# Attention and mixture of experts on one core: the fifth score tile of each unit laid over its two PSUM banks as 384 and 256 columns

## The chip, the cores and the metric

The kernel runs on one core of a Trainium2 chip. The metric is the device time of one execution, in microseconds, as the median of several runs. The program has one launch and no arithmetic on the host beyond repacking of weights. TensorE is PE below, its weight loads are PEld, VectorE is DVE, ScalarE is ACT, GpSimd is POOL, SyncE is SP.

## What is computed

A layer norm feeds two branches, whose sum is added to the input: causal attention with rotary positions (2 batches, 1024 tokens, 16 heads of 128), and a mixture of 32 experts with a shared expert, which takes the same normalised tokens. The change touches the attention's scores alone. Cut to what matters:

```python
q = rope((x @ wq.T + bq).reshape(b, s, 16, 128))        # b = 2, s = 1024
k = rope((x @ wk.T + bk).reshape(b, s, 16, 128))
v = (x @ wv.T + bv).reshape(b, s, 16, 128)
attn = jnp.einsum('bihd,bjhd->bhij', q, k) * scale
attn = jnp.where(causal[None, None], -jnp.inf, attn)     # j > i is masked
attn = jax.nn.softmax(attn, axis=-1)
o = jnp.einsum('bhij,bjhd->bihd', attn, v).reshape(b, s, 2048)
y = o @ wo.T + bo + residual
```

## The kernel before

**Units.** One head of one batch is a unit; there are 32 (`UNITS`), numbered n, and the program is a loop over them after a prologue (layer norm, transposes, the shared expert, the gate). In the loop every engine has its work written out by hand in a fixed order, and semaphores tie the engines together. The stages of neighbouring units overlap: while the scores of unit n are made, the second half of unit n-1 is weighted with its values and projected out, and the rotary inputs of unit n+1 are projected. From unit 13 on, sixteen units also carry a pair of experts each (`expert_turn`, `expert_up`, `expert_down`).

**Precision by three products.** Most operands are held as a high and a low part, and `three` (L284 to L287) issues three matmuls for one product: high by high (L285), high by low (L286), low by high (L287). Each of these has its own weights, so every matmul comes with a weight load. In the rows a group by L285, L286, L287 of the same width is one such product. The rows name the stationary and the moving operand after the arrow; the form ends in the number of columns that are moved, so `128x384` is 384 columns.

**Scores.** A unit has eight score tiles, t = 0 to 7. Tile t holds 128 queries against the (t + 1) x 128 keys that the causal mask lets through. `scores` (L383) makes it in PSUM. A PSUM bank holds 512 columns of 4 bytes; `score[0]` is banks 0 and 1 joined, `score[1]` banks 2 and 3, and tile t lies in `score[t % 2]` from column 0 on. One matmul can't cross a bank, so tiles 0 to 3 are one piece and tiles 4 to 7 are two: 512 columns in the first bank, and 128, 256, 384 or 512 in the second. Behind the pieces a bf16 matmul (L399) adds the mask to the last 128 columns and signals `s_done`.

**What follows a tile.** DVE takes the negated maximum of each row over the whole tile (L1388, `nmax`), ACT the exponential with it as bias and the row sum (L959, `prob`), then PE transposes `prob` in groups of up to four blocks (L409, `turn`) into one of four ring banks (banks 4 to 7, `take`), from which ACT makes the high part (L970, `ptd_h` or `ptr_h`) and DVE the low one (L1397). These are the moving operands of `weighted`. The score tile t waits for the exponential of tile t - 2, which empties its banks.

**The order on PE around tile 4.** In unit n it is: the second half of unit n-1 is weighted, in the expert units the gathered tokens are transposed (`expert_turn`, L456), then `scores(n, 4)`, `project(n + 1, 2)`, `turn(n, 3)`, `project(n + 1, 3)`, `scores(n, 5)`, `outproj(n - 1, 1, 0)`, `turn(n, 4)`, `scores(n, 6)`.

**The rotary chain.** `project` makes q and k of the next unit; ACT copies them with their bias into `qb` (L759, L763); SP swaps their two halves by DMA into `qs` (`swap`); POOL multiplies with cosine and sine and adds (L1525, L1526, L1529); ACT and POOL or DVE make high and low parts (L772, L1073). `scores(n, 0)` and `scores(n, 4)` wait for them.

Of the kernel before, what the change touches and what calls it, by code (L numbers as in the profile page):

```python
# [10 lines left out]
ALU = mybir.AluOpType  # L11
ACT = mybir.ActivationFunctionType
AX = mybir.AxisListType

P = 128
# [4 lines left out]
TILES = SEQ // P  # L20
CH = 512
# [61 lines left out]
def layer(nc, x, wqk, wvp, wop, biases, epack, gate_wt, gate_bias, sh_gate, sh_up, sh_down, cols, bo_row, cst, out):  # L83
# [9 lines left out]
    with ExitStack() as ctx:  # L93
        def sb(name, shape, dt=F32, where=ctx):
            return where.enter_context(nc.sbuf_tensor(name, shape, dt))
# [3 lines left out]

        ps = ctx.enter_context(nc.psum_tensor("ps", [P, 8, CH], F32))  # L100
        score = [ps[:, 2 * i:2 * i + 2, :].rearrange("p a b -> p (a b)") for i in range(2)]

        k_sb = sb("k_sb", [P, C_END])
        ident, cos_sb, sin_sb = k_sb[:, C_ID:C_ID + P], k_sb[:, C_COS:C_COS + SEQ], k_sb[:, C_SIN:C_SIN + SEQ]
# [2 lines left out]
        bias = sb("bias", [P, 3 * HEADS])  # L107
# [71 lines left out]
        prob = sb("prob", [P, 2, SEQ])  # L179
        nmax, rsum, rinv = sb("nmax", [P, TILES]), sb("rsum", [P, TILES]), sb("rinv", [P, TILES])  # L180
# [103 lines left out]
        def three(eng, dst, lhs, rhs, start, stop):  # L284
            eng.matmul(dst, lhs[0], rhs[0], start=start, stop=False)  # L285
            eng.matmul(dst, lhs[0], rhs[1], start=False, stop=False)  # L286
            return eng.matmul(dst, lhs[1], rhs[0], start=False, stop=stop)  # L287

        @block.tensor
        def _(pe):  # L290
# [92 lines left out]
            def scores(n, t):  # L383
                if n not in range(UNITS):
                    return
                if n == 0 and t in (0, 1, 4, 5):
                    i = 2 * (t % 2) + t // 4
                    pe.wait_ge(pro_free[i], len([u for u in range(len(pro_uses)) if u % 4 == i]))
                if not (n == 0 and t < 2):
                    pe.wait_ge(exp_done, TILES * n + t - 1)  # L390
                if t % 4 == 0:
                    pe.wait_ge(rope_l, 4 * n + (2, 4)[t // 4])
                s = n % 2
                dst, i = score[t % 2], slice(t * P, (t + 1) * P)
                for c in range(t // 4 + 1):
                    w = min(CH, (t + 1) * P - c * CH)
                    j = slice(c * CH, c * CH + w)
                    three(pe, dst[:, j], (q_h[s][:, i], q_l[s][:, i]), (k_h[s][:, j], k_l[s][:, j]), True, c < t // 4)
                pe.matmul(dst[:, t * P:(t + 1) * P], maskb[:, 0:P], maskb[:, P:2 * P], start=False,  # L399
                          stop=True).then_inc(s_done, 1)  # L400
# [157 lines left out]

            for n in range(UNITS):
                scores(n, 0)  # L560
                turn(n - 1, 8)
                turn(n - 1, 9)
                if n > 1:
                    values(n - 1, 2)
                scores(n, 1)
                if n > 1:
                    values(n - 1, 3)
                turn(n - 1, 10)
                expert_down(n - 1)
                turn(n - 1, 11)  # L570
                project(n + 1, 1)
                scores(n, 2)
                masks(n, 0)
                bias_row(n)
# [227 lines left out]
        def _(act):  # L802
# [151 lines left out]
            def exps(n, t):  # L954
                if n not in range(UNITS):
                    return
                act.wait_ge(max_done, TILES * n + t + 1)
                w = (t + 1) * P
                act.activation(prob[:, t % 2, 0:w], score[t % 2][:, 0:w], ACT.Exp, bias=nmax[:, t:t + 1],  # L959
                               accum_out=rsum[:, t:t + 1]).then_inc(exp_done, 1)  # L960

            def turned_hi(n, g):
# [46 lines left out]
            for n in range(UNITS):  # L1009
                g = n // 4  # L1010
                exps(n, 0)
                turned_hi(n - 1, 11)
                expert_out(n - 1)
                exps(n, 1)
                rope_in(act, n + 1, 1)
                masks(n, 0)
                bias_row(n)
                turned_hi(n, 0)
                turned_hi(n, 1)
                masks(n, 1)  # L1020
                exps(n, 2)
                rope_hi(act, n + 1, 0)
                turned_hi(n, 2)
# [79 lines left out]
        def _(dve):  # L1103
# [280 lines left out]
            def maxes(n, t):  # L1384
                if n not in range(UNITS):
                    return
                dve.wait_ge(s_done, TILES * n + t + 1)
                dve.tensor_reduce(nmax[:, t:t + 1], score[t % 2][:, 0:(t + 1) * P], AX.X, ALU.max,  # L1388
                                  negate=True).then_inc(max_done, 1)

            def turned_lo(n, g):
# [59 lines left out]
            for n in range(UNITS):  # L1451
                g = n // 4
                if n == 1:
                    dve.memset(ones[:, :], 1.0).then_inc(ones_ready, 1)
                maxes(n, 0)
                if n > 1:
                    v_lo(dve, n - 1, 2)
                maxes(n, 1)
                if n > 1:
                    v_lo(dve, n - 1, 3)  # L1460
                turned_lo(n - 1, 10)
                turned_lo(n - 1, 11)
                add_out(n - 1, 0, 0)
                turned_lo(n, 0)
                maxes(n, 2)
                add_out(n - 1, 0, 1)
                add_rest(n, 0)
# [219 lines left out]
```

## Time and profile before

| what | us |
|---|---|
| median of 3 runs | 1086.73 |
| the three runs | 1086.23, 1086.73, 1088.49 |
| the profiled execution | 1089.67 |
| its span, from the first instruction to the last | 1087.8 |
| PE busy in it | 1046.8 (96%) |
| POOL, DVE, ACT busy in it | 749.5, 719.7, 658.6 |

The profiled execution is one execution of its own, with a span from the first to the last instruction; the numbers of the trace are of this one. The busy time of PE is modelled at its end: a matmul's shown duration holds its way through the array, and successive matmuls overlap. How long a full PE takes for a matmul is the distance between the starts of two rows. The chain of work is a list of pieces, each from the time at which its releaser was done.

### The profile page before, as it was taken

Reading aid. Unit: us, or ns where it says so; the run is one execution under the profiler, and the core shown is the slowest. Engines: PE = TensorE matmul, PEld = TensorE weight load, DVE = VectorE, ACT = ScalarE, POOL = GpSimd, SP = SyncE. Lnnn points to the kernel's source line nnn. Section 1 sums busy time; section 2 is a strip of 40 time slices with the busy share of each in tenths; the row PEclk is TensorE's granted clock in tenths of the full one; section 3 lists DMA queues with packets and bytes.
Section 4 is the critical chain, followed back from the end, with each engine's and each line's share of the span. In section 5 each row is a group of like instructions: output and inputs, shape, how many; then the busy total and the mean of one; then the engine's idle time right before and its main releaser. Section 6 shows DMA issues by size and latency. Waiting matters only on the chain.

```text
span 1087.8 us, 19027 instructions
## 1 busy us (share of the span) xinstructions
PE 1046.8 (96%) x6738; PEld 917.8 (84%) x6738; DVE 719.7 (66%) x1489; ACT 658.6 (61%) x1448; POOL 749.5 (69%) x654
## 2 busy tenths in 40 slices
PE   3999999999999999999999999999999999999996
PEld 3888888888878888888988888898888889888885
DVE  5867778778778766656665565666566556656575
ACT  3577656666665656656665566666556666656552
POOL 3826776767766575768678687867867877685751
PEclk9999999999999999999999999999999999999999
DMA  6221416212121211223332232332223232222112
GB/s 231 59 64 39 117 40 116 60 28 48 43 58 35 54 41 39 59 69 73 87 93 48 67 80 69 96 81 70 64 65 98 61 84 55 72 64 48 41 59 97
DMA packets 51629, 75.43 MB, mean 69 GB/s; under 512 B 12240, under 2 KB 29008, under 8 KB 51408
## 3 DMA queue, kind: packets, MB, share of 16 engines
q1 hardware_dynamic: 46144, 67.66, 23.7%
q0 software_dynamic: 5392, 6.56, 4.1%
q8 instruction: 55, 0.90, 0.4%
q14 instruction: 38, 0.31, 0.1%
HBM read 33.94 MB, written 10.90 MB: 41 GB/s over the span
## 4 chain that ended last, share of the span: by engine, by line
PE 79%; POOL 8%; DVE 4%; DMA 3%; ACT 3%; issue 2%; SPq 0%; DVEq 0%; POOLq 0%; ACTq 0%
PE ps L285 22%; PE ps L287 21%; PE ps L286 21%; PE ps L409 10%; PE ps L470 2%; DMA qs<-qb 2%; POOL qs L1526 2%; POOL qb L1529 2%; POOL qb L1525 2%; PE ps L399 1%; PE ps L482 1%; DMA fin_y<-token_sum 1%; DVE acc L1421 1%; POOL q_l L1073 1%; DVE nmax L1388 1%
## 5 line engine op out<-in xcount | busy, mean ns | idle before, releaser
L1525 POOL TENSOR_TENSOR qb<-qb,k_sb 128x512 f32<-128x512 f32 x128 | 170.9, 1336 | 236.3 <-DMA qs<-qb 235.9
L1388 DVE TENSOR_REDUCE nmax<-ps 128x1 f32<-128x128 f32 (+7 forms) x256 | 191.0, 752 | 63.9 <-PE ps L399 63.6
L959 ACT ACTIVATE prob<-ps,nmax 128x128 f32<-128x128 f32 (+7 forms) x256 | 190.3, 743 | 61.9 <-DVE nmax L1388 61.1
L970 ACT ACTIVATE ptd_h<-ps 128x128 fp32r<-128x128 f32 (+3 forms) x256 | 108.7, 436 | 191.1 <-PE ps L409 190.6
L1397 DVE TENSOR_TENSOR ptd_l<-ps,ptd_h 128x128 fp32r<-128x128 f32 (+3 forms) x256 | 124.6, 487 | 84.3 <-ACT ptd_h L970 81.4
L1529 POOL TENSOR_TENSOR qb<-qb,qs 128x512 f32<-128x512 f32 x128 | 165.8, 1295 | 19.0 <-POOL qs L1526 1.0
L409 PE MATMUL ps<-k_sb,prob 128*128 128x128 f32 x1152 | 172.7, 274 | 6.2 <-DVE ptr_l L1397 3.9
L1526 POOL TENSOR_TENSOR qs<-qs,k_sb 128x512 f32<-128x512 f32 x128 | 172.9, 1351 | 0.0
L409 PEld LDWEIGHTS ps<-k_sb,prob 128*128 128x128 f32 x1152 | 132.8, 141 | 18.5 <-issue 7.3
L285 PE MATMUL ps<-k_h,q_h 128*128 128x512 f32 (+3 forms) x384 | 140.9, 367 | 4.1 <-ACT prob L959 3.6
L1421 DVE SCALAR_TENSOR_TENSOR acc<-ps,rinv,acc 128x256 f32<-128x256 f32 x256 | 111.1, 476 | 33.9 <-PE ps L287 33.9
L287 PE MATMUL ps<-k_h,q_l 128*128 128x512 f32 (+3 forms) x384 | 132.7, 346 | 0.0
L286 PE MATMUL ps<-k_l,q_h 128*128 128x512 f32 (+3 forms) x384 | 132.6, 345 | 0.0
L285 PE MATMUL ps<-x2h,wqh 128*128 128x512 f32 x256 | 111.4, 435 | 5.4 <-DVE acc L1421 5.2
L287 PE MATMUL ps<-x2h,wql 128*128 128x512 f32 x256 | 100.7, 393 | 0.0
L286 PE MATMUL ps<-x2l,wqh 128*128 128x512 f32 x256 | 100.4, 392 | 0.0
L1397 DVE TENSOR_TENSOR ptr_l<-ps,ptr_h 128x512 fp32r<-128x512 f32 x128 | 87.6, 684 | 11.3 <-ACT ptr_h L970 11.0
L970 ACT ACTIVATE ptr_h<-ps 128x512 fp32r<-128x512 f32 x128 | 75.9, 593 | 21.4 <-PE ps L409 21.4
L285 PEld LDWEIGHTS ps<-k_h,q_h 128*128 128x128 f32 x384 | 72.5, 189 | 16.7 <-ACT prob L959 7.1
L1073 POOL TENSOR_TENSOR q_l<-qb,q_h 128x512 fp32r<-128x512 f32 x62 | 80.4, 1296 | 6.1 <-ACT q_h L772 5.8
L285 PE MATMUL ps<-ptd_h,v_h 128*128 128x512 f32 (+3 forms) x256 | 84.2, 329 | 0.0
L287 PE MATMUL ps<-ptd_h,v_l 128*128 128x512 f32 (+3 forms) x256 | 82.7, 323 | 0.0
(175 smaller groups left out, 2668.5 us busy)
## 6 DMA issues: line engine op xcount, KB each, us to landing
qs<-qb SPq DMA_DIRECT2D x256, 128.0 KB
ew<-epack SPq DMA_DIRECT2D x16, 768.0 KB, 4.3
rqk<-wqk SPq DMA_DIRECT2D x16, 256.0 KB, 3.0
xt<-x SPq DMA_DIRECT2D x4, 512.0 KB, 5.0
rv<-wvp SPq DMA_DIRECT2D x8, 256.0 KB, 3.3
ro<-wop SPq DMA_DIRECT2D x16, 128.0 KB, 2.3
token_table<-xn SPq DMA_DIRECT2D x4, 512.0 KB, 4.7
token_sum<-token_table SPq DMA_DIRECT2D x1, 2048.0 KB, 9.1
```

The source lines that it names most:

```text
L285: eng.matmul(dst, lhs[0], rhs[0], start=start, stop=False)
L286: eng.matmul(dst, lhs[0], rhs[1], start=False, stop=False)
L287: return eng.matmul(dst, lhs[1], rhs[0], start=False, stop=stop)
L409: ins = pe.transpose(bank[:, j * P:(j + 1) * P], prob[:, t % 2, (j0 + j) * P:(j0 + j + 1) * P], ident)
L959: act.activation(prob[:, t % 2, 0:w], score[t % 2][:, 0:w], ACT.Exp, bias=nmax[:, t:t + 1], accum_out=rsum[:, t:t + 1]).then_inc(exp_done, 1)
L970: act.activation(turned(0, t, j0, w), src, ACT.Copy).then_inc(pth_done, 1)
L1388: dve.tensor_reduce(nmax[:, t:t + 1], score[t % 2][:, 0:(t + 1) * P], AX.X, ALU.max, negate=True).then_inc(max_done, 1)
L1397: dve.tensor_tensor(turned(1, t, j0, w), src, turned(0, t, j0, w).bitcast(F32), ALU.subtract).then_inc(ptl_done, 1)
L1421: ins = dve.scalar_tensor_tensor(out=acc[:, t, :], in0=rbank("OP", u, c, i2)[:, i * DM:(i + 1) * DM], scalar=rinv[:, j:j + 1], in1=acc[:, ...
L1525: pool.tensor_tensor(qb[:, i, :], qb[:, i, :], cos_sb[:, c], ALU.mult).then_inc(rope_a, 1)
L1526: pool.tensor_tensor(qs[:, i % 2, :], qs[:, i % 2, :], sin_sb[:, c], ALU.mult).then_inc(rope_b, 1)
L1529: pool.tensor_tensor(qb[:, i, :], qb[:, i, :], qs[:, i % 2, :], ALU.add).then_inc(rope_t, 1)
```

## The change

The fifth score tile (t = 4, 640 keys) no longer starts at column 0 of its pair of banks but at column 128, and so takes columns 128 to 767: 384 in the first bank and 256 in the second, in place of 512 and 128. A list `tile` holds the view of each of the eight tiles; the others are where they were. `mid` is the number of columns of the first piece, 384 at t = 4 and 512 elsewhere. The maximum and the exponential read the new view. In `scores` the three matmuls of each piece take the widths that follow from it. No instruction is added, removed or moved.

```diff
+        tile = [score[t % 2][:, P * (t == 4):P * (t == 4) + (t + 1) * P] for t in range(TILES)]
...
-                dst, i = score[t % 2], slice(t * P, (t + 1) * P)
+                dst, i = tile[t], slice(t * P, (t + 1) * P)
+                mid = CH - P * (t == 4)
                 for c in range(t // 4 + 1):
-                    w = min(CH, (t + 1) * P - c * CH)
-                    j = slice(c * CH, c * CH + w)
+                    j = slice(c * mid, min((t + 1) * P, mid + c * CH))
                     three(pe, dst[:, j], (q_h[s][:, i], q_l[s][:, i]), (k_h[s][:, j], k_l[s][:, j]), True, c < t // 4)
...
-                act.activation(prob[:, t % 2, 0:w], score[t % 2][:, 0:w], ACT.Exp, bias=nmax[:, t:t + 1],
+                act.activation(prob[:, t % 2, 0:w], tile[t], ACT.Exp, bias=nmax[:, t:t + 1],
...
-                dve.tensor_reduce(nmax[:, t:t + 1], score[t % 2][:, 0:(t + 1) * P], AX.X, ALU.max,
+                dve.tensor_reduce(nmax[:, t:t + 1], tile[t], AX.X, ALU.max,
```

On PE, at the tile t = 4 of one unit, the order before has these rows (`k_h,q_h` and its like are keys moved against the stationary queries):

```order
L285 MATMUL ps<-k_h,q_h 128x512
L286 MATMUL ps<-k_l,q_h 128x512
L287 MATMUL ps<-k_h,q_l 128x512
L285 MATMUL ps<-k_h,q_h 128x128
L286 MATMUL ps<-k_l,q_h 128x128
L287 MATMUL ps<-k_h,q_l 128x128
L399 MATMUL ps<-maskb 128x128
```

and with the change, in the same place (its lines stand two further down):

```order
L287 MATMUL ps<-k_h,q_h 128x384
L288 MATMUL ps<-k_l,q_h 128x384
L289 MATMUL ps<-k_h,q_l 128x384
L287 MATMUL ps<-k_h,q_h 128x256
L288 MATMUL ps<-k_l,q_h 128x256
L289 MATMUL ps<-k_h,q_l 128x256
L401 MATMUL ps<-maskb 128x128
```

Only the widths differ, at all 32 tiles; the rows of the other engines keep their order and their forms.

## Rows read from the trace of the kernel before

**Rows 1.** The page, parts 1 and 2: PE's busy time, granted clock by slice

```profile
PE 1046.8 (96%) x6738; PEld 917.8 (84%) x6738; DVE 719.7 (66%) x1489; ACT 658.6 (61%) x1448; POOL 749.5 (69%) x654
...
PEclk9999999999999999999999999999999999999999
```

**Rows 2.** The page, part 4: shares of the chain that ended last

```profile
PE 79%; POOL 8%; DVE 4%; DMA 3%; ACT 3%; issue 2%; SPq 0%; DVEq 0%; POOLq 0%; ACTq 0%
```

**Rows 3.** Timeline of PE, unit 14, tile 4: start us, duration us, engine, line, tiles

```profile
511.94 0.48 PE L285 MATMUL ps<-k_h,q_h 128*128 128x512 f32 x1
512.25 0.40 PE L286 MATMUL ps<-k_l,q_h 128*128 128x512 f32 x1
512.49 0.39 PE L287 MATMUL ps<-k_h,q_l 128*128 128x512 f32 x1
512.72 0.22 PE L285 MATMUL ps<-k_h,q_h 128*128 128x128 f32 x1
512.77 0.28 PE L286 MATMUL ps<-k_l,q_h 128*128 128x128 f32 x1
512.89 0.27 PE L287 MATMUL ps<-k_h,q_l 128*128 128x128 f32 x1
513.00 0.23 PE L399 MATMUL ps<-maskb 128*128 128x128 bf16 x1
```

**Rows 4.** Timeline of the weight loads, the same tile, second piece

```profile
512.72 0.19 PEld L286 LDWEIGHTS ps<-k_l,q_h 128*128 128x128 f32 x1
512.83 0.19 PEld L287 LDWEIGHTS ps<-k_h,q_l 128*128 128x128 f32 x1
```

**Rows 5.** The chain in order of time (start us, us, what): one expert up projection

```profile
491.77 1.73 PE ps L470 x16
```

**Rows 6.** Timeline of PE, unit 14, tile 5: its first matmul, its second piece's, its mask

```profile
516.36 0.39 PE L285 MATMUL ps<-k_h,q_h 128*128 128x512 f32 x1
...
517.04 0.28 PE L285 MATMUL ps<-k_h,q_h 128*128 128x256 f32 x1
...
517.39 0.23 PE L399 MATMUL ps<-maskb 128*128 128x128 bf16 x1
```

**Rows 7.** Timeline of PE, unit 14, tile 2: its first matmul and its mask

```profile
503.56 0.33 PE L285 MATMUL ps<-k_h,q_h 128*128 128x384 f32 x1
...
504.08 0.23 PE L399 MATMUL ps<-maskb 128*128 128x128 bf16 x1
```

**Rows 8.** Timeline of ACT and of PE, unit 14: exponential of tile 4, its transposes

```profile
516.24 0.80 ACT L959 ACTIVATE prob<-ps,nmax 128x640 f32<-128x640 f32 x1
...
518.22 0.49 PE L409 MATMUL ps<-k_sb,prob 128*128 128x128 f32 x3
```

**Rows 9.** The chain in order of time, unit 3, around the routing work

```profile
179.87 0.69 DVE ol L1410
...
188.28 0.47 PE ps L285
```

**Rows 10.** The chain in order of time, unit 8

```profile
329.48 0.61 ACT oh L976
...
343.19 0.47 PE ps L285
```

**Rows 11.** The chain in order of time, last unit: the final additions

```profile
1051.34 1.14 DVE acc L1449
...
1069.36 1.15 DVE nmax L1388
```

**Rows 12.** The chain in order of time, unit 25 into 26: the rotary chain

```profile
872.97 3.58 DMA qs<-qb
...
887.35 0.30 ACT q_h L772
...
891.46 0.41 PE ps L409 x2
```

**Rows 13.** The chain in order of time, unit 0: another swap of the rotary halves

```profile
97.93 2.31 DMA qs<-qb
```

## Prediction

> **What bounds the kernel now.** I read four views, in this order. First the page: TensorE (PE) is busy for 96% of the span, at full granted clock in every slice [rows 1], so no clock effect hides in the time. Second, the chain of work that ended last: 79% of its length is PE [rows 2]. A busy share alone would prove little, since matmuls overlap in the trace and their ends are modelled; that the chain runs through PE is what makes a shorter PE stream worth something. Third, the timeline of PE around one fifth score tile (t = 4), in unit 14 [rows 3]. The reader is to look at the first column and not at the second: a matmul of 128 columns is shown with 0.22 to 0.28 us and one of 512 with 0.39 to 0.48 us, yet they start 0.23 us apart after a 512 and closer after a 128. What a matmul costs on a full PE is the distance from its start to the next start. Fourth, the chain in order of time, asked at each of the 32 tiles t = 4, to see which of them lie on it.
>
> **What 512 and 128 cost.** In [rows 3] the tile runs from 511.94 to its mask matmul at 513.00: 1.06 us. The three matmuls of 512 take 511.94 to 512.72, 0.78 us: 0.31 for the first, which follows transposes and has to make up for a late weight load, then 0.24 and 0.23. The three of 128 take 512.72 to 513.00, 0.28 us, in steps of 0.05, 0.12 and 0.11. A column costs 0.23/512 = 0.45 ns in the wide ones, so 128 columns are worth 0.06 us, and only the first of the three gets that. The other two stand at 0.11 to 0.12. The weight loads say why: the second and the third one of the narrow piece start at 512.72 and 512.83, 0.11 us apart [rows 4]. Each of these matmuls has its own weights, the next load can't start before the one ahead is done, and a matmul shorter than 0.11 us is waited out. That this floor doesn't come from the columns is shown elsewhere: 16 matmuls of the experts' up projection, 64 columns wide, take 1.73 us in one piece of the chain, again 0.108 us each [rows 5]. So some 0.11 us per tile are PE time in which no column moves.
>
> **What 384 and 256 cost.** Both widths stand in the trace of before. Three of 256, as the second piece of t = 5, take 517.04 to 517.39, 0.35 us or 0.117 each [rows 6]: just above the floor, so they hide their weight loads and pay almost only for their columns. Three of 384, the whole of t = 2, take 503.56 to 504.08, 0.52 us or 0.173 each [rows 7]. Of 512 three steady ones cost 3 x 0.233 = 0.70 by the steps of 0.24 and 0.23 in [rows 3]. The edits, for one tile:
> - first piece, 512 to 384: minus 0.70 - 0.52 = 0.18 us (the three of 512 in the tile t = 5 beside it run from 516.36 to 517.04, 0.68 [rows 6], by which it would be 0.16);
> - second piece, 128 to 256: plus 0.35 - 0.28 = 0.07 us;
> - the same six matmuls and six weight loads, the same 640 columns, the same mask of 128 columns at the end of the second bank, nothing moved in any engine's order: 0.
> Sum: minus 0.11, or minus 0.09 with the 0.16. I take 0.105, since 0.18 is what the steps beside the tile itself give, rounded down a little for the other end. The first matmul after transposes isn't seen with 384 columns and the short weights ahead. Its bounds: it shrinks by its columns (0.06, in the sum) or, if its 0.31 were all weight load, not at all, which would leave 0.045 per tile. I take the first, because it takes 0.08 more than a steady 512, and a fixed extra with the columns on top fits that; the low end is kept for the range.
>
> VectorE's maximum and ScalarE's exponential read the tile from column 128 to 768 in place of 0 to 640, over the same two banks. The form is the same 640 elements, and before, too, they step over a bank's end in the middle; I price this at 0. No row shows a read that begins inside a bank; if it cost something, the cover is this: the exponential of t = 4 runs from 516.24 for 0.80 us, and PE turns that tile from 518.22 on [rows 8], so over 1 us is free. Without this cover it would fall on the transposes' start.
>
> **How many of the 32 tiles count.** At 29 of them the chain consists of PE's matmuls of this very tile. The three others: in unit 3 the chain has gone to VectorE, with `ol` at 179.87 and then routing work up to PE's restart at 188.28 [rows 9], and the tile t = 4 stands beside it; in unit 8 it leaves PE for ScalarE's `oh` at 329.48, before the tile is done, and is back at 343.19 [rows 10]; in the last unit it runs over the final additions and their loads, from 1051.34 to 1069.36 [rows 11], with the tile beside them. There PE, being earlier, only waits longer. So the term is 29 x 0.105 = 3.05 us, and 32 x 0.105 = 3.4 would be the most.
>
> What is late next? The rotary chain: PE's projection, ScalarE's copy, the swap by DMA, GpSimd's products, ScalarE, PE. After the tile of unit 25 the chain takes that way, from the DMA at 872.97 to PE at 891.46 [rows 12]. The projections that start it stand behind the tile t = 4 in PE's order, and no other t = 4 stands between its start and its end, so an earlier tile moves the whole chain forward and the gain survives it.
>
> The sum is made against the profiled execution, 1089.67 us with a span of 1087.8, so 1.9 us lie outside and stay. It is 2.9 us above the median of the runs, about as far as the highest of them; the difference is carried over to the median: 1086.73 - 3.05 = **1083.7 us**, a ratio of 0.997.
>
> **Rivals.** (a) A matmul costs by its columns and nothing else. Then 3 x 640 columns stay 3 x 640 columns, and the time is 1086.7. For it: wide matmuls follow their columns closely. Against it: the steps of 0.11 and 0.12 for 128 columns [rows 3] and 0.108 for 64 [rows 5]. The Trainium skill has such a rule: TensorE: Matmul & The Clock Gate, section "Back-to-back issue gap", gives an isolated gap of columns / 2.4 plus 2.5 ns, by which both layouts cost alike; the same section says that weight loads push narrow matmuls above it, with 81 ns at 128 columns and 131 at 512, between which a straight line would again make the two layouts equal. The steps of 0.11 and 0.23 us here agree with neither pair, and the measurement decides.
> (b) Part of the gain ends in waits: a second path, nearly as long as the chain, that doesn't pass the tile. Where three units do this visibly, ten more might with the margin of a tenth of a microsecond; or the low bound of 0.045 per tile holds. 29 x 0.045 = 1.3, time 1085.4. For it: VectorE and ScalarE each form a queue in fixed order, and the chain visits them between units. Against it: the view of waits names no wait of a matmul in the stretch of the 16 expert units, so nothing there holds PE up now.
> (c) Slower: the swap of the rotary halves shares its queue with the experts' weights, the largest of the loads. It takes 3.58 us at 872.97 but 2.31 at 97.93 [rows 12, 13]. With PE a tenth earlier in each unit, swaps may meet loads that they missed before; ScalarE then stands at `q_h` until GpSimd is done, with the copies that PE needs queued behind it. The price is at most 3.58 - 2.31 = 1.27 us per unit. Two such units eat the gain, and from five on the kernel is slower by more than 2.2 us: 5 x 1.27 - 3.05 = 3.3, time 1090.0. Against it: the load is itself released by PE's steps, so the two keep their distance.
> (d) The widths aren't what the change says. The order of the built kernel shows 384 and 256 at the tiles and nothing else changed. 1086.7.
>
> **How the numbers follow.** Forecast 0.72; (a) 0.07; (b) 0.14; (c) 0.06; (d) 0.01. The bound of 0.2%, about what a measurement of this kernel can tell from no change, is 2.2 us, so faster means under 1084.6. The forecast's own range is 1082.6 (3.4 saved, and 0.7 of scatter, a little over the 0.5 between the two lower runs) to 1085.0; I put 0.65 of its 0.72 under 1084.6 and 0.07 above. Faster 0.65; same 0.07 + 0.14 + 0.07 + 0.01 = 0.29; slower 0.06. The range that should hold 8 in 10 runs from 1082.6 to 1086.4: it takes in (b) with its bound, and leaves out (c), most of (a) and (d), and the forecast's tails, together 0.18.
>
> **What would show it.** In the profile after: the tile t = 4 of unit 14 in about 0.95 us from first matmul to mask, with steps of 0.25, 0.17, 0.17, 0.12, 0.12, 0.12; its weight loads nowhere closer than the matmuls; the tiles' reads as long as before; the distance between the same tiles of neighbouring expert units shorter by 0.1 us. If the tile is shorter and the span isn't, it is (b), and new waits of PE stand behind ScalarE or VectorE. If the steps of 256 are above 0.12, or the 384s above 0.18, the sum per tile is wrong. Longer swaps at ScalarE's `q_h` would be (c).

## The result

| | median us | lowest to highest | runs |
|---|---|---|---|
| before | 1087.93 | 1085.24 to 1090.75 | 22 |
| after | 1085.33 | 1083.14 to 1087.09 | 22 |

The ratio is 0.9978, with a 95% interval of 0.997 to 0.9986: 2.4 us faster (1.5 to 3.3). The profiled execution of after has a span of 1083.6 us, 4.2 us less than that of before; that difference of two single executions holds more than the change, as is worked out further down.

The page of after, parts 1 and 4, against [rows 1, 2]:

```profile
PE 1043.6 (96%) x6738; PEld 918.5 (85%) x6738; DVE 720.2 (66%) x1489; ACT 659.0 (61%) x1448; POOL 748.9 (69%) x654
...
PE 84%; POOL 5%; DVE 4%; DMA 3%; ACT 2%; issue 1%; SPq 0%; DVEq 0%; POOLq 0%; ACTq 0%
```

PE's busy time is 3.2 us less; those of VectorE, ScalarE and GpSimd have moved by 0.6 us at most. The tile t = 4 of unit 14 on the timeline of PE (start us, duration us, engine, line, tiles), against [rows 3]:

```profile
511.48 0.42 PE L287 MATMUL ps<-k_h,q_h 128*128 128x384 f32 x1
511.74 0.33 PE L288 MATMUL ps<-k_l,q_h 128*128 128x384 f32 x1
511.91 0.34 PE L289 MATMUL ps<-k_h,q_l 128*128 128x384 f32 x1
512.09 0.28 PE L287 MATMUL ps<-k_h,q_h 128*128 128x256 f32 x1
512.20 0.28 PE L288 MATMUL ps<-k_l,q_h 128*128 128x256 f32 x1
512.32 0.28 PE L289 MATMUL ps<-k_h,q_l 128*128 128x256 f32 x1
512.45 0.23 PE L401 MATMUL ps<-maskb 128*128 128x128 bf16 x1
```

From first matmul to mask it is 0.97 us against 1.06, in steps of 0.26, 0.17, 0.18, 0.11, 0.12, 0.13. The gain is carried on from unit to unit. The first matmul of the tile in units 13 and 20, two rows of before and then two of after:

```profile
482.79 0.48 PE L285 MATMUL ps<-k_h,q_h 128*128 128x512 f32 x1
704.20 0.48 PE L285 MATMUL ps<-k_h,q_h 128*128 128x512 f32 x1
```

```profile
482.44 0.42 PE L287 MATMUL ps<-k_h,q_h 128*128 128x384 f32 x1
703.14 0.42 PE L287 MATMUL ps<-k_h,q_h 128*128 128x384 f32 x1
```

221.41 us against 220.70 for seven units: 0.10 us per unit, and nothing of it is given back there. But at the start of this stretch after is only 0.35 us ahead, where the thirteen units before it should have brought 1.3. The place is unit 8: from the mask matmul of its tile 3 to that of unit 9 it is 35.92 us in before and 36.97 in after. The waits of PE in it on its timeline (in brackets the idle time before a row and what ended it), before first, then after:

```profile
340.12 0.39 PE L285 MATMUL ps<-wvh,x2h 128*128 128x256 f32 x1 [0.49 <-DVE acc L1421]
343.19 0.47 PE L285 MATMUL ps<-x2h,wqh 128*128 128x512 f32 x1 [1.08 <-DVE acc L1421]
```

```profile
340.18 0.38 PE L287 MATMUL ps<-wvh,x2h 128*128 128x256 f32 x1 [1.62 <-DVE acc L1423]
343.24 0.47 PE L287 MATMUL ps<-x2h,wqh 128*128 128x512 f32 x1 [1.08 <-DVE acc L1423]
```

One wait has grown from 0.49 to 1.62 us. What VectorE and GpSimd did just ahead of it, in before:

```profile
336.51 0.47 DVE L1098 SCALAR_TENSOR_TENSOR cacc<-ro,bias,cacc 128x256 f32<-128x256 f32 x1
336.56 1.57 POOL L1525 TENSOR_TENSOR qb<-qb,k_sb 128x512 f32<-128x512 f32 x1 [7.58 <-DMA qs<-qb]
336.90 1.50 DVE L1100 TENSOR_TENSOR wol<-ro,woh 128x256 fp32r<-128x256 f32 x1
```

and in after:

```profile
335.48 1.28 POOL L1527 TENSOR_TENSOR qb<-qb,k_sb 128x512 f32<-128x512 f32 x1 [7.48 <-DMA qs<-qb]
335.54 1.50 DVE L1100 SCALAR_TENSOR_TENSOR cacc<-ro,bias,cacc 128x256 f32<-128x256 f32 x1
...
336.96 1.51 DVE L1102 TENSOR_TENSOR wol<-ro,woh 128x256 fp32r<-128x256 f32 x1
```

The same addition on VectorE, `cacc`, takes 0.47 us where it begins 0.05 us ahead of GpSimd's product, and 1.50 where it begins 0.06 behind it. That is 1.03 us of VectorE's queue, at one of the places where the chain runs over VectorE. GpSimd's product waits for the swap of the rotary halves, and begins 2.88 or 2.89 us after the swap's first DMA is issued. That issue on SyncE's queue, before and then after:

```profile
333.68 0.46 SPq L652 DMA_DIRECT2D qs<-qb  x1
332.59 0.46 SPq L654 DMA_DIRECT2D qs<-qb  x1
```

From it to the start of `cacc` it is 2.83 us in before and 2.95 in after: the swap comes 0.12 us sooner against VectorE's queue.

### The profile page after: what moved, and what is told of

Read it like the earlier page. It is cut to its first block, busy times and chain, and to the rows that moved or that the text cites. A ratio compares the mean times of both kernels' runs of the same rounds, so it can differ in the third digit from the quotient of the medians.

```text
span 1083.6 us, 19027 instructions
## 1 busy us (share of the span) xinstructions
PE 1043.6 (96%) x6738; PEld 918.5 (85%) x6738; DVE 720.2 (66%) x1489; ACT 659.0 (61%) x1448; POOL 748.9 (69%) x654
## 4 chain that ended last, share of the span: by engine, by line
PE 84%; POOL 5%; DVE 4%; DMA 3%; ACT 2%; issue 1%; SPq 0%; DVEq 0%; POOLq 0%; ACTq 0%
PE ps L287 23%; PE ps L289 22%; PE ps L288 22%; PE ps L411 10%; PE ps L472 2%; DMA qs<-qb 1%; PE ps L401 1%; POOL qb L1531 1%; PE ps L484 1%; POOL qb L1527 1%; POOL qs L1528 1%; DVE acc L1423 1%; DMA fin_y<-token_sum 1%; DVE nmax L1390 1%; POOL q_l L1075 1%
## 5 line engine op out<-in xcount | busy, mean ns | idle before, releaser
L782 ACT ACTIVATE v_h<-ps 128x512 fp32r<-128x512 f32 x64 | 38.1, 597 | 73.7 <-PE ps L289 73.6
```

## The experiments

Ten variants, and the kernels before and after once more each. Where a distance per unit is given, it runs from the mask matmul of tile 3 in unit 13 to that in unit 19, divided by six. In before:

```profile
477.51 0.23 PE L399 MATMUL ps<-maskb 128*128 128x128 bf16 x1
...
669.77 0.23 PE L399 MATMUL ps<-maskb 128*128 128x128 bf16 x1
```

This is 192.26 us, or 32.04 per unit; in after it is 31.94. The second traces of these two kernels give the same within 0.01 us. For a kernel that has one execution only, the trace is used and the time is not.

**w448: 448 and 192 columns.** After, with the offset and the cut changed:

```diff
-score[t % 2][:, P * (t == 4):P * (t == 4) + (t + 1) * P]
+score[t % 2][:, 64 * (t == 4):64 * (t == 4) + (t + 1) * P]
...
-                mid = CH - P * (t == 4)
+                mid = CH - 64 * (t == 4)
```

> Tile 4 laid as 448 and 192 columns (offset 64). Load theory: a matmul with its own weights can't follow the one ahead closer than the 0.11 us between two weight loads, and pays 0.45 ns per column where that is more. 192 columns are worth 0.09 us, so the second and third of the narrow piece still stand at 0.11 to 0.12; the tile of unit 14 takes about 1.01 us from first matmul to mask, half way between 1.06 (before) and 0.97 (after). Rival, columns only: the same as in both kernels, which differ already. Rival, it is the bank's layout and not the width (the tile no longer starts at a bank's first column): 0.97 at once, since this one, too, starts inside the bank. Total about 1.5 us below before by the load theory, too little to be told from one time; the trace decides.

Measured: the tile of unit 14 takes 1.01 us, from 512.85 to 513.86. The narrow piece on PE's timeline:

```profile
513.54 0.25 PE L287 MATMUL ps<-k_h,q_h 128*128 128x192 f32 x1
513.63 0.28 PE L288 MATMUL ps<-k_l,q_h 128*128 128x192 f32 x1
513.74 0.28 PE L289 MATMUL ps<-k_h,q_l 128*128 128x192 f32 x1
513.86 0.23 PE L401 MATMUL ps<-maskb 128*128 128x128 bf16 x1
```

The steps are 0.09, 0.11 and 0.12: from the second on, 192 columns pay what 128 pay. It starts inside the bank and yet doesn't have the whole gain in the tile, 0.05 us of 0.09. The distance per unit is 31.96 us, which is 0.08 of the 0.10, so by that measure the lack is only 0.02, and w448 alone doesn't settle whether the place in the bank pays. w128 does.

**w320: 320 and 320 columns**, with 192 in place of 64.

> Tile 4 laid as 320 and 320 columns (offset 192). Load theory: both widths are above the floor, so nothing is gained over 384 and 256: tile 0.95 to 0.97 us in unit 14, steps of 0.145 each behind the first. Rival, the balance of the two pieces is what pays: from 512/128 by way of 384/256 to 320/320 the gain goes on, half as much again, tile about 0.92. Total as after, within its scatter.

Measured: 511.49 to 512.46, 0.97 us as in after, with steps of 0.14 to 0.15 behind the first. The distance per unit is 31.93 us, 0.01 below after. Once both widths are above the floor of 0.11 us, evening them out brings no more than that.

**w128: 128 columns first, 512 behind**, with 384 in place of 64.

> Tile 4 mirrored, 128 columns first and 512 behind (offset 384). Load theory: the three narrow matmuls stand at 0.11 each wherever they are, so the tile takes 1.04 to 1.07 us in unit 14 as before, and the total is that of before, ratio 0.999 to 1.001. Rival, what paid in the change was that the tile starts inside its bank or that its mask lies in a well filled bank: then this one, which has both, keeps the gain: 0.97 and ratio 0.9978.

Measured: ratio to before 1.0008 (0.9999 to 1.0018), 1089.67 us against 1088.52. The gain is gone, as the load theory has it and the rival doesn't. But the size was off: the tile takes 1.12 us (512.39 to 513.51), not 1.04 to 1.07, and the distance per unit is 0.05 us above that of before. Its middle on the timeline:

```profile
512.65 0.27 PE L289 MATMUL ps<-k_h,q_l 128*128 128x128 f32 x1
512.76 0.45 PE L287 MATMUL ps<-k_h,q_h 128*128 128x512 f32 x1
513.04 0.40 PE L288 MATMUL ps<-k_l,q_h 128*128 128x512 f32 x1
513.28 0.40 PE L289 MATMUL ps<-k_h,q_l 128*128 128x512 f32 x1
```

A 512 that follows a narrow one has 0.28 us to the next start, where 0.23 or 0.24 is usual.

**mixed: 512 and 128 as before, the matmuls of the two pieces in turn.**

```diff
+                if t == 4:
+                    for m, (qx, kx) in enumerate(((q_h, k_h), (q_h, k_l), (q_l, k_h))):
+                        for j in (slice(0, CH), slice(CH, CH + P)):
+                            pe.matmul(dst[:, j], qx[s][:, i], kx[s][:, j], start=m == 0, stop=m == 2 and j.start == 0)
```

> Tile 4 in the layout of before, 512 and 128 columns, but the matmuls of the two pieces alternate: wide, narrow, wide, narrow, wide, narrow. Load theory: the load behind a narrow matmul runs on under the wide one that follows, so a narrow one costs 0.06 us: steps 0.31, 0.06, 0.23, 0.06, 0.23, 0.06, tile 0.95 us, as good as 384 and 256 without changing the layout; total ratio 0.997 to 0.998. Rival, narrow matmuls have a price of their own, 0.11 us whatever stands beside them: tile 1.06 to 1.11 us, ratio 1.000 or above.

Measured: ratio to before 1.0006 (0.9997 to 1.0016). My expectation fell. The tile takes 1.07 us, as in before (wide and narrow are merged in a row, x2):

```profile
512.31 0.54 PE L398 MATMUL ps<-k_h,q_h 128*128 128x512 f32 x2
512.68 0.50 PE L398 MATMUL ps<-k_l,q_h 128*128 128x512 f32 x2
513.02 0.51 PE L398 MATMUL ps<-k_h,q_l 128*128 128x512 f32 x2
513.38 0.23 PE L403 MATMUL ps<-maskb 128*128 128x128 bf16 x1
```

A pair takes 0.34 us, which is 0.23 + 0.11. So the step of 0.06 behind a lone narrow matmul, also in [rows 3], is only in the shown starts: the 512 behind it gives the other 0.05 back, as in w128. The refined form of the theory, made after these runs to fit them: a matmul holds PE for the longer of its own columns and the load of the weights **behind** it, 0.11 us for the ones used here. Neither order nor neighbours help against that, with one exception, the mask. The load of its bf16 weights is shown with 0.10 us, where the others are shown with 0.19 [rows 4]; in after:

```profile
512.45 0.10 PEld L401 LDWEIGHTS ps<-maskb 128*128 128x128 bf16 x1
```

By this form the narrow matmul ahead of the mask costs 0.06. In before that is the third narrow one; in w128 it is a 512, which has no use for it, and so w128 loses those 0.05. It gives w448 a gain of 0.07 us per tile (three of 448 at 0.20, two of 192 at 0.11 and the last at 0.09, 0.91 against 0.98), between the 0.05 of its tile and the 0.08 of its distance.

**nmask: the narrow piece and its mask first, then the 512.**

```diff
+                    j = slice(CH, CH + P)
+                    three(pe, dst[:, j], (q_h[s][:, i], q_l[s][:, i]), (k_h[s][:, j], k_l[s][:, j]), True, False)
+                    pe.matmul(dst[:, j], maskb[:, 0:P], maskb[:, P:2 * P], start=False, stop=True)
+                    j = slice(0, CH)
+                    three(pe, dst[:, j], (q_h[s][:, i], q_l[s][:, i]), (k_h[s][:, j], k_l[s][:, j]), True,
+                          True).then_inc(s_done, 1)
```

> The layout of before (512 and 128 columns), but the narrow piece and its mask are issued first and the wide piece last. Refined load theory, after the runs with the order turned: a matmul holds PE for the longer of its own columns (0.45 ns each) and the load of the weights behind it, 0.11 us for the usual ones and 0.06 at most for the mask's bf16 ones; so two narrow ones cost 0.11, and the one ahead of the mask 0.06. Here the mask again stands behind a narrow one, so the distance between the same tiles of neighbouring units is that of before, within 0.02 us. Rival, a narrow piece in front costs more because it stands behind the transposes: the distance grows by 0.05 us per unit, as it did with 128 columns first and the mask last.

Measured, by the mask of tile 3 in units 13 and 19:

```profile
476.64 0.23 PE L407 MATMUL ps<-maskb 128*128 128x128 bf16 x1
...
668.80 0.23 PE L407 MATMUL ps<-maskb 128*128 128x128 bf16 x1
```

That is 32.03 us per unit, 0.02 below before, where w128 with 32.09 is 0.05 above. Both have the narrow piece in front; what differs is what stands behind its last matmul. The refined form holds, the rival doesn't.

**five: five pieces of 128 columns.**

```diff
-                for c in range(t // 4 + 1):
-                    j = slice(c * mid, min((t + 1) * P, mid + c * CH))
+                cuts = [P * c for c in range(6)] if t == 4 else [c * mid for c in range(t // 4 + 1)] + [(t + 1) * P]
+                for a, b in zip(cuts, cuts[1:]):
+                    j = slice(a, b)
```

> The layout of after, but tile 4 cut into five pieces of 128 columns, 15 matmuls in place of 6. Load theory: twelve more narrow matmuls at 0.111 us in place of three of 512 at 0.233, against before plus 0.63 us per tile, and so in the distance between neighbouring units. If 29 tiles lie on the path that sets the end, the total is 18.4 us above before (ratio 1.0169); if all 32 count, 20.3 us (1.0186). Rival, columns only: the tile would be as in the fully used layout, about 0.1 us below before.

Measured: 0.63 us per unit over before, exactly the price. Mask of tile 3 in unit 13, and in unit 19 the same 196.06 us later, against 192.26 in before:

```profile
483.92 0.23 PE L402 MATMUL ps<-maskb 128*128 128x128 bf16 x1
```

The total is 1.0151 times before (1.0129 to 1.0173), 16.4 us, so 26 tiles' worth (22 to 30), below the 18.4 us of 29 tiles but with it inside the interval; the 20.3 us of all 32 lie outside. The trace shows where the dose is missing. From the mask of tile 3 to that of the next unit, 23 of the 31 distances are 0.62 to 0.67 us above those of before, and three are more (units 2, 3 and 19, by 0.89 to 1.26). Units 7, 8, 21, 25 and 29 pay nothing or little: 0.94, 0.54 and 0.10 below, 0.12 above, 1.02 below. In units 7, 21, 25 and 29 the chain of before goes over a rotary swap of 3.58 to 4.13 us, and that of five over none; in unit 8 PE's longest wait behind VectorE's additions is 0.80 us instead of 1.08. So a large dose seems to eat waits that 0.1 us doesn't. Part of it may be chance, since unit 7 is 1.74 us shorter in after2 than in before, too.

**again: the kernel before, a second trace.**

> The kernel before once more, for its trace. Question: in unit 8 the span of after lost 1.0 us against before, since one addition on VectorE (cacc) took 1.50 us in place of 0.48 beside a product on GpSimd that had begun 0.06 us ahead of it; in the trace of before the product began 0.05 us behind it. Theory, phase: with 0.1 us of jitter in the swap's DMA either may happen in either kernel, so cacc may be long here too, and unit 8 then takes 1.0 us more than in the first trace. Rival: the earlier tile 4 causes it; then cacc is short here, 0.48 us.

Measured: `cacc` in unit 8 is short, 0.47 us, and from unit 13 to 19 the two traces of before agree within 0.01 us. So the rival of this expectation is the one that fits: it doesn't look like a toss of a coin, as far as one more trace can say. All traces that keep `cacc` at its place and have the product beside it, by the time from the issue of the swap to `cacc` in unit 8:

| kernel | swap to `cacc`, us | product begins | `cacc`, us |
|---|---|---|---|
| w128 | 2.76 | 0.12 later | 0.47 |
| before | 2.83 | 0.05 later | 0.47 |
| old8 (below) | 2.83 | 0.06 later | 0.48 |
| again | 2.84 | 0.04 later | 0.47 |
| nmask | 2.85 | 0.03 later | 1.60 |
| mixed | 2.85 | 0.02 later | 1.58 |
| w448 | 2.91 | 0.03 earlier | 1.53 |
| t5even (below) | 2.93 | 0.05 earlier | 1.52 |
| after, after2, w320 | 2.95 | 0.06 to 0.07 earlier | 1.50 |

The order is that of the distance per unit, from 32.09 us in w128 to 31.93 in w320 (old8 has the old tile in this unit), and `cacc` turns from short to long between 0.04 and 0.03 us. The kernel before stands right beside this edge: mixed and nmask, whose units are only 0.01 to 0.02 us shorter than its, are already on the long side.

**late8: after, `cacc` and `wol` of unit 8 further down VectorE's order.**

```diff
-                if n % 4 == 0 and n:
+                if n % 4 == 0 and n not in (0, MASKS):
                     wo_lo(dve, 2 * g)
...
                 add_out(n - 1, 1, 1)
+                if n == MASKS:
+                    wo_lo(dve, 2 * g)
```

> After, with one step of VectorE's order moved in unit 8 alone: the two operations on the output weights (cacc and wol) stand behind the second half of the projection's additions, where PE doesn't wait for them. Theory: PE's waits in unit 8 (1.62 and 1.08 us in the trace of after, 0.49 and 1.08 in that of before) are VectorE's queue, so they shrink by what leaves the queue ahead of them, 1.9 to 3.0 us, down to nothing at most: unit 8 shorter than in after by 1.6 to 2.7 us, total 1.6 to 2.7 us below after, ratio to before 0.9953 to 0.9963. Rival, PE's wait comes from the routing scan of 4.4 us and the transposes behind it: no more than 0.5 us gained.

Measured: 1084.50 us against 1088.26 for before, run beside it, ratio 0.9966 (0.9956 to 0.9976), just above the range that was expected. The 1.62 us of waiting are gone, but a wait came up further down, on PE's timeline:

```profile
338.75 0.47 PE L287 MATMUL ps<-x2h,wqh 128*128 128x512 f32 x1 [0.74 <-DVE acc L1423]
```

```profile
346.27 0.30 PE L411 MATMUL ps<-k_sb,prob 128*128 128x128 f32 x1 [1.08 <-DVE ptr_l L1399]
```

Of the 2.70 us in after, 1.82 are left. From the mask of tile 3 in unit 8 to that in unit 9 it is 35.82 us against 36.97 in after, 1.15 less, where 1.6 to 2.7 were expected.

**after2: after once more.**

> The kernel after once more, beside the variants of this call. Theory, phase: in unit 8 the rotary product on GpSimd starts 0.12 us sooner against VectorE's cacc than in before, since the swap is issued sooner by what tile 4 saves; it then stands ahead of cacc, which takes 1.50 us in place of 0.48. So cacc is long here too, unit 8 takes 1.0 us more than in before, and the total is as measured before: ratio 0.997 to 0.9986. Rival, chance: cacc is short, and unit 8 as in before.

Measured: 1085.43 us against 1088.52, ratio 0.9975 (0.9965 to 0.9986). `cacc` is long, 1.50 us, and PE's wait 1.62, as in the first trace.

**old8: after, but the old layout in unit 8** (`OLD` is 8; `mid` follows it).

```diff
+        def tile(n, t):
+            o = P * (t == 4 and n != OLD)
+            return score[t % 2][:, o:o + (t + 1) * P]
```

> After, with the old layout of tile 4 in unit 8 alone. Phase theory: the product there starts 0.12 us later again, behind cacc, which takes 0.48 us; unit 8 is 1.0 us shorter than in after, although its tile 4 is 0.1 us longer, and the total 1.0 us below after, ratio to before 0.9967 to 0.9972. Rival, chance: no difference to after but 0.1 us more in unit 8.

Measured, in unit 8:

```profile
333.95 0.48 DVE L1103 SCALAR_TENSOR_TENSOR cacc<-ro,bias,cacc 128x256 f32<-128x256 f32 x1
334.01 1.57 POOL L1530 TENSOR_TENSOR qb<-qb,k_sb 128x512 f32<-128x512 f32 x1 [7.58 <-DMA qs<-qb]
334.35 1.51 DVE L1105 TENSOR_TENSOR wol<-ro,woh 128x256 fp32r<-128x256 f32 x1
```

`cacc` is short again and the product behind it; PE's wait is 0.49 us in place of 1.62, and the distance over unit 8 is 35.97 us in place of 37.03 in after2. One tile of 0.1 us, put back, returns 1.0 us in the trace. Together with after2, beside which it ran, and the table above, that shows what lengthens unit 8 in the traces. In the total it doesn't show: 1085.35 against 1085.43 us, ratio 0.9972 (0.996 to 0.9983), whose interval holds both the ratio of after2 and one microsecond less. The loss of 1.0 us of time stays a reading of the traces.

**later8: `cacc` and `wol` of unit 8 behind transposed blocks 6 and 7.**

```diff
                 turned_lo(n, 7)
+                if n == MASKS:
+                    wo_lo(dve, 2 * g)
                 out_lo(n, 0)
```

> After, with cacc and wol of unit 8 moved still further down VectorE's order than in late8, behind its transposed blocks 6 and 7. In late8 one wait of PE of 1.08 us for VectorE's ptr_l came up where none had been. Theory: it is the 2.2 us of cacc and wol that stand ahead of it, so it goes, and unit 8 gets about 1.0 us shorter than in late8: total 3.5 to 4.8 us below before, ratio 0.9956 to 0.9968. Rival: the search of the routing (2.3 us) ahead of it keeps PE waiting; then the wait stays and the time is that of late8, 0.9966.

Measured: 1083.92 us, ratio 0.9960 (0.9945 to 0.9974). The wait for `ptr_l` is gone, as expected, and a smaller one has taken its place:

```profile
348.79 0.38 PE L287 MATMUL ps<-wvh,x2h 128*128 128x256 f32 x1 [0.54 <-DVE ol L1412]
```

The distance over unit 8 is 35.33 us, 0.5 less than in late8, where about 1.0 was expected; the total is inside its range. It has the lowest median here. Against before the interval is clear; against after2, which ran beside it, the difference is 1.5 us and the intervals overlap, so that it beats after is likely and not shown.

**t5even: after, and tile 5 as 384 and 384 columns.**

```diff
-P * (t == 4):P * (t == 4) + (t + 1) * P
+P * (t in (4, 5)):P * (t in (4, 5)) + (t + 1) * P
...
-                mid = CH - P * (t == 4)
+                mid = CH - P * (t in (4, 5))
```

> After, and tile 5 laid as 384 and 384 columns in place of 512 and 256. Load theory: all three widths are above the floor, so the tile's time stays, 1.04 us in unit 14 within 0.02, and the units keep their length. Rival, even pieces are better as such: tile 5 shorter by 0.05 us or more.

Measured: tile 5 of unit 14 from its first row to its mask takes 1.05 us, as in before (1.03, [rows 6]) within the 0.02, and the distance per unit is 31.95 us against 31.94 in after:

```profile
514.22 0.33 PE L287 MATMUL ps<-k_h,q_h 128*128 128x384 f32 x1
...
515.27 0.23 PE L401 MATMUL ps<-maskb 128*128 128x128 bf16 x1
```

## Why the prediction was right, point by point

**The price of the layout: right.** 0.105 us per tile was forecast; the distance per unit fell by 0.10. The steps forecast for the new tile (0.25, 0.17, 0.17, 0.12, 0.12, 0.12) came within 0.01. Its reason was right too, that a narrow matmul waits for a weight load; the low bound of 0.045 wasn't needed, the first matmul shrank by 0.05, about its columns.

**The time: inside the wide range, above the forecast's own.** The median of 1085.33 us is 1.6 above the 1083.7 forecast and 0.3 above the upper end of 1085.0. Most of that is the base: the median of three runs, 1086.73, lay 1.2 us below that of the 22, 1087.93. That the profiled execution lay about as far from this median as the highest run was misread, too: it is 2.9 us above, the highest run 1.8. The gain itself, 2.4 us (1.5 to 3.3), holds the forecast 3.05 in its interval, and doesn't settle whether it is more than the 2.2 us from which on the prediction says faster. Rival (b) with the low bound gives 1085.4, almost the measured median, but only through the base: its gain of 1.3 us lies outside the interval, and its 0.045 per tile is measured at 0.10.

**The reads of the tile: right.** The exponential of tile 4 in unit 14 takes 0.80 us in after, as in [rows 8], although it starts inside a bank.

**How the floor works: half right.** The prediction said that only the second and the third narrow matmul pay it and that the first gets by with 0.06 us, by the shown starts. mixed and w128 show that the first pays 0.11 like the second, and that it is the last one, ahead of the mask, which is cheap. Since that, too, makes two that pay, the sum came out the same; to this extent the right price was luck. That a load can't start before the one ahead is done isn't seen in [rows 4] either: loads of 0.19 us are shown there 0.11 apart, so they overlap as shown. What the rows show is the spacing.

**How many tiles count: 29 forecast.** From the mask of tile 3 to that of the next unit, after is 0.07 to 0.13 us shorter than before in 25 of the 31 distances, 2.6 us together. The six others are units 3, 7, 8, 21, 25 and 29, with changes of -0.32, -0.06, +1.05, -0.58, +0.09 and -1.15 us. Unit 8 is the next point; in the other five, single executions scatter too much for a tenth to be read: there the two traces of before differ by 0.05 to 0.34 us. Unit 31, whose end has no such mask, isn't read. Through five the total says 26, with an interval from 22 to 30.

**The loss in unit 8: missed.** The prediction had unit 8 as a tile that doesn't count, its gain lost in PE's wait. In fact it costs: the swap is issued 0.12 us sooner against `cacc`, GpSimd's product comes in front of it, and VectorE loses 1.03 us on the chain. after2 has it and old8 doesn't. So, with the 29 as forecast, the sum reads 29 x 0.10 = 2.9, less 1.0, which is 1.9 us; measured are 2.4 (1.5 to 3.3). Rival (c), something that meets because PE is a tenth early, was right as a kind, but named the wrong pair and the wrong place. The forecast gain was 0.65 us too high. Unit 8 would more than explain it, but the interval is wider than this difference, so that isn't shown in the total.

**Rival (a), columns only,** is out: all these kernels move 1920 columns per tile in their score products, and the tile of unit 14 takes 0.97, 1.01, 1.06 or 1.12 us by their cut and order, and 1.71 in five. The isolated gap of the Trainium skill (TensorE: Matmul & The Clock Gate, section "Back-to-back issue gap") leaves out the load, and the 81 and 131 ns that the same section gives for 128 and 512 columns aren't found here, where 0.11 and 0.23 us stand.

**Rival (b), the gain lost in waits:** not in the expert units. The view of waits of after, for PE from 483 to 1010 us, has a single line (waiter, releaser, us in total, times, longest):

```profile
PE ps L411 <- ACT qb L761: 0.2, 1, 0.2
```

**The span's 4.2 us.** By the medians 2.4 belong to the change. Between the two traces 25 distances give the 2.6 us, and unit 8 takes 1.05 back; units 21 and 29 give 0.58 and 1.15, where a tile is worth a tenth. In unit 29 the swap took 4.08 us in before and 3.04 in after, and the distance over the unit is 28.49 us against 27.34. In the chain in order of time, before and then after:

```profile
1001.43 4.08 DMA qs<-qb
```

```profile
999.12 3.04 DMA qs<-qb
```

In unit 7 the distance is 28.98 us in before, 28.92 in after and 27.24 in after2, so one and the same kernel has both. For unit 29 that is less clear: the swap on the chain took 3.21 to 4.08 us in the five traces without the shorter tile (before, again, mixed, nmask, w128), and 3.03 to 3.62 in the eight with it. Rival (c) looked for longer swaps; none of the kind shows, and whether a part of the gain is shorter ones was not tested.

## What to carry to other kernels

Where every matmul brings its own weights, cut work into pieces whose columns take at least as long as the next weight load. Here that is about 256 columns, with 4-byte operands at full granted clock; above that the cut doesn't matter, and alternating wide and narrow ones doesn't help. Read prices from the distance of starts over a whole group, not from a single step behind a narrow matmul. And a saving of a tenth of a microsecond can cost ten times that elsewhere, by changing which of two engines gets going first: look for places where two of them start within a tenth of each other ahead of a wait.

## What the runs showed of the hardware that was not expected

VectorE and GpSimd, both on operands in SBUF, hold each other up by who begins first. In unit 8 `cacc` took 0.47 to 0.48 us when it began 0.04 us or more ahead of a product on GpSimd, and 1.50 to 1.60 when it began 0.03 ahead or less, or behind; `wol`, which follows, took 1.50 beside the product and takes 0.42 in a unit where none runs. The rows of after in the next unit that has both:

```profile
367.98 0.48 DVE L1100 SCALAR_TENSOR_TENSOR cacc<-ro,bias,cacc 128x256 f32<-128x256 f32 x1
```

```profile
368.38 0.42 DVE L1102 TENSOR_TENSOR wol<-ro,woh 128x256 fp32r<-128x256 f32 x1
```

The one that comes second waits the other out. In all seven traces with a long `cacc` it ends 0.28 or 0.29 us after GpSimd's product, and in the four with a short one the product takes 1.50 to 1.58 us in place of 1.28 and ends 1.15 after `cacc`. In late8, where `cacc` stands further down, it began 0.83 us behind another operation of GpSimd, and again ended 0.28 after it, on GpSimd's timeline and then VectorE's:

```profile
337.70 1.27 POOL L1075 TENSOR_TENSOR q_l<-qb,q_h 128x512 fp32r<-128x512 f32 x1 [0.30 <-ACT q_h L774]
```

```profile
338.53 0.72 DVE L1100 SCALAR_TENSOR_TENSOR cacc<-ro,bias,cacc 128x256 f32<-128x256 f32 x1
```

Which of their shared means they wait for wasn't tried.

The start shown for a matmul behind a narrow one lies about 0.05 us too early. In [rows 3] the first narrow matmul has 0.05 us to the next start, and in w128 the 512 behind a narrow one has 0.28, where 0.11 and 0.23 are the rule; a pair of 128 and 512 columns takes 0.34 together in mixed, which is the sum of either reading.
